# Layout of a DRAM scratch tensor in a CIN tower: one 8 KB row per partition for the loads, eight 512-byte rows per partition for the stores

## The reference

```python
e = stack([tbl_f[ids[:, f]] for f in range(64)], axis=1)        # 512 x 64 x 16
x = e; outs = []
for W, b in ((W0, b0), (W1, b1), (W2, b2)):
    z = einsum('bhd,bfd->bhfd', x, e).reshape(B, h * f, d)
    x = einsum('oc,bcd->bod', W, z) + b[None, :, None]
    outs.append(x.sum(axis=2))
h = concatenate(outs + [dense_ctx], axis=1)
y = relu(relu(h @ W_top1 + b_top1) @ W_top2 + b_top2) @ W_top3
```

## Time and profile before

| | |
|---|---|
| median of 3 runs | 1180.73 us (1180.33 to 1181.44) |
| the profiled execution's own time | 1183.49 us |
| its span in the trace | 1181.5 us |
| busy share PE / DVE / POOL / ACT | 95% / 84% / 77% / 58% |
| mean granted clock of TensorE | 0.994 |
| transfers: packets, bytes | 103836, 142.87 MB |

### The profile page before, as it was taken

One profiled execution on the slowest core, in us unless ns is written; L12 is line 12 of the kernel. 1 busy time (PEld: TensorE's weight loads), 2 busy tenths in 40 slices (PEclk: granted clock), 3 DMA queues, 4 the chain that ended last, 5 costly groups with the idle time before them and its releaser, 6 DMA issues.

```text
span 1181.5 us, 13928 instructions
## 1 busy us (share of the span) xinstructions
PE 1117.9 (95%) x4276; PEld 745.3 (63%) x4276; DVE 997.4 (84%) x652; ACT 681.9 (58%) x695; POOL 905.2 (77%) x403
## 2 busy tenths in 40 slices
PE   0499999999999999999999999999999999999998
PEld 0256666666666666676666666666666666667685
DVE  4589899989998989899899989898998999896542
ACT  5256465665656656656656566566566665654533
POOL 6459998889988888888899888888898996575000
PEclk9999999999999999999999999999999999999999
DMA  6542424234252524252342525241523425242991
GB/s 240 170 130 65 113 74 150 65 120 121 77 155 74 157 74 140 68 152 66 109 131 71 160 74 157 74 140 64 146 76 104 136 69 160 73 152 94 294 297 46
DMA packets 103836, 142.87 MB, mean 121 GB/s; under 512 B 11745, under 2 KB 55009, under 8 KB 103042
## 3 DMA queue, kind: packets, MB, share of 16 engines
q1 hardware_dynamic: 95618, 140.42, 39.3%
q0 software_dynamic: 8192, 2.11, 2.2%
HBM read 114.96 MB, written 27.53 MB: 121 GB/s over the span
## 4 chain that ended last, share of the span: by engine, by line
PE 83%; POOL 4%; issue 3%; DMA 3%; SPq 2%; ACT 2%; DVE 1%; ACTq 0%
PE acc L1085 50%; PE acc L1079 26%; POOL z_lo L580 3%; PE turn_gram_ps L1153 3%; DMA z_float<-gram_scratch 2%; PE acc L1108 1%; POOL emb L571 1%; ACT x L878 1%; DMA z<-gram_scratch 1%; PE z_ps L1214 1%; PE turn_gram_ps L1140 1%; DMA land<-x_scratch 1%; ACT z_hi L1046 0%; DVE z_lo L816 0%; SPq L512 0%
## 5 line engine op out<-in xcount | busy, mean ns | idle before, releaser
L580 POOL TENSOR_TENSOR z_lo<-z,z_hi 128x2048 fp32r<-128x2048 f32 x143 | 659.5, 4613 | 116.8 <-ACT z_hi L849 110.3
L1085 PE MATMUL acc<-z_hi,w_hi 128*128 128x512 f32 x896 | 379.0, 423 | 6.8 <-DVE z_lo L659 4.2
L1079 PE MATMUL acc<-z_float,w_sb 128*128 128x512 f32 x768 | 349.1, 601 | 8.2 <-ACT x L878 7.6
L1085 PE MATMUL acc<-z_hi,w_lo 128*128 128x512 f32 x896 | 354.6, 396 | 0.0
L1085 PE MATMUL acc<-z_lo,w_hi 128*128 128x512 f32 x896 | 354.3, 395 | 0.0
L849 ACT ACTIVATE z_hi<-z 128x2048 fp32r<-128x2048 f32 x144 | 275.1, 1910 | 53.6 <-DVE z L647 53.6
L571 POOL DMA_INDIRECT emb<-in_tables,rows_chunk x256 | 245.4, 959 | 63.3 <-issue 51.8
L1079 PEld LDWEIGHTS acc<-z_float,w_sb 128*128 128x128 f32 x768 | 144.4, 191 | 174.6 <-issue 166.4
L858 ACT ACTIVATE z_hi<-z_ps 128x1024 fp32r<-128x1024 f32 x160 | 164.9, 1031 | 135.9 <-PE acc L1085 108.9
L659 DVE TENSOR_TENSOR z_lo<-z_ps,z_hi 128x1024 fp32r<-128x1024 f32 x160 | 194.9, 1218 | 45.3 <-ACT z_hi L858 45.3
L647 DVE TENSOR_TENSOR z<-operand_even,x_shift 128x2048 f32<-128x2048 f32 x80 | 183.0, 2287 | 37.3 <-PE acc L1085 16.6
(11 more groups left out here) (112 smaller groups left out, 640.7 us busy)
## 6 DMA issues: line engine op xcount, KB each, us to landing
land<-x_scratch SPq DMA_DIRECT2D x128, 256.0 KB
land<-x_scratch SPq DMA_DIRECT2D x128, 128.0 KB
x_shift<-x_scratch SPq DMA_DIRECT2D x16, 1024.0 KB, 5.8
gram_scratch<-gram SPq DMA_DIRECT2D x32, 512.0 KB
x_shift<-x_scratch SPq DMA_DIRECT2D x16, 768.0 KB
z_float<-gram_scratch SPq DMA_DIRECT2D x7, 1024.0 KB, 10.8
x_scratch<-emb SPq DMA_DIRECT2D x32, 192.0 KB
x_shift<-gram_scratch SPq DMA_DIRECT2D x6, 1024.0 KB, 9.2
```

The source lines that it names most:

```text
L580: pool.tensor_tensor(z_lo[:, slot], z[:, slot], z_hi[:, slot].bitcast(F32), ALU.subtract).then_inc(subtracted, 1)
L1079: mm = pe.matmul(acc[:, :], weights[:, tile0 + q, :], z_float[:, g.float_slot(pos), q, :], start=start and q == 0, stop=stop and q == QUAD ...
L1085: mm = pe.matmul(acc[:, :], w[:, tile, :], zz[:, slot, q, :], start=False, stop=stop and n == 2)
```

## The change

The scratch tensor in DRAM gets another order of dimensions. Before, each partition (channel h) had for each of the 32 chunk halves all 64 fields. After, each partition has for each of the 8 blocks of fields all 32 chunk halves. Both tensors have the same size, and the step from one partition to the next is the same, 128 KiB. The store of a half has the same bytes from the same buffer, but its 4096 bytes per partition now go to 8 places in DRAM, 16 KiB apart. The load of a block has the same bytes to the same buffer, but its 8192 bytes per partition now come from one place rather than from 16 places 4 KiB apart. Nothing else changes: order, waits, semaphores, buffers and arithmetic stay.

```diff
-    gram_scratch = nc.dram_tensor("gram_scratch", (HID, 2 * CHUNKS, FIELDS, HALF_B), F32, kind="Internal").ap()
+    gram_scratch = nc.dram_tensor("gram_scratch", (HID, HALF_BLOCKS, 2 * CHUNKS, F_BLOCK * HALF_B), F32, kind="Internal").ap()
@@ store_gram
-                offset, = at(c.count(2 * FIELDS * HALF_B, half * FIELDS * HALF_B))
+                offset, = at(c.count(2 * F_BLOCK * HALF_B, half * F_BLOCK * HALF_B))
                 wait_all((gram_staged, c.count(BLOCKS, 2 * half + 2)))
                 sp.dma_start(bass.AP(gram_scratch.tensor, offset,
-                                     [[2 * CHUNKS * FIELDS * HALF_B, HID], [1, FIELDS * HALF_B]]),
-                             gram[:, :, :].rearrange("p f b -> p (f b)")).then_inc(gram_stored, 16)
+                                     [[2 * CHUNKS * FIELDS * HALF_B, HID], [2 * CHUNKS * F_BLOCK * HALF_B, HALF_BLOCKS],
+                                      [1, F_BLOCK * HALF_B]]),
+                             gram[:, :, :].rearrange("p (k f) b -> p k (f b)", f=F_BLOCK)).then_inc(gram_stored, 16)
@@ load_gram
-                sp.dma_start(gram_buffers[k % GRAM_BUFFERS].rearrange("p c f b -> p c (f b)"), bass.AP(
-                    gram_scratch.tensor, (half * CHUNKS * FIELDS + fb * F_BLOCK) * HALF_B,
-                    [[2 * CHUNKS * FIELDS * HALF_B, HID], [FIELDS * HALF_B, CHUNKS], [1, F_BLOCK * HALF_B]],
+                sp.dma_start(gram_buffers[k % GRAM_BUFFERS].rearrange("p c f b -> p (c f b)"), bass.AP(
+                    gram_scratch.tensor, (fb * 2 + half) * CHUNKS * F_BLOCK * HALF_B,
+                    [[2 * CHUNKS * FIELDS * HALF_B, HID], [1, CHUNKS * F_BLOCK * HALF_B]],
                 )).then_inc(gram_loaded[k % GRAM_BUFFERS], 16)
```

## The result

The changed kernel takes 1173.72 us (median of 4 runs, 1172.88 to 1173.98) against 1181.09 us of the kernel before in the same session (1180.33 to 1181.76): a ratio of 0.9936, 95% interval 0.9923 to 0.9948. The profiled execution took 1172.88 us, with a span of 1170.9 us. The lines of the new kernel have moved by one behind the store: L1225 is what L1224 was, L1047 what L1046 was, L513 what L512 was.

What follows compares the result with a forecast made beforehand. PE bounds the rounds, the saturated load queue the last layer. Faster loads give 5.3 us less 0.1 for handovers, stores nothing: 1180.73 less 5.2 gives 1175.5 us (profiled 1183.49 to 1178.3), range 1174.3 to 1179.5.

Steps and rivals of the forecast that it cites:

- What bounds the last layer, and what comes next: Last layer: the saturated DMA queue bounds it at 290 GB/s; with faster loads PE sets the end, at 1160.9 us.
- The load at 2.5 us: Last layer's 16 scratch loads: each takes 2.5 us in 8192-byte rows, against 3.62 us at 290 GB/s.
- together 45.5 us: PE's work in the last layer from the first split block: 12 split blocks of 3.20 us plus two plain, 7.1 us.
- 5.3 us, is all that faster loads can give: Last layer: PE's 50.8 us less 45.5 us of its own work, the upper limit of the gain.
- about 0.9 us of slow clock: Last layer: part of the 5.3 us, beside 4.4 us of gaps; PE's clock was 0.62 between 1136 and 1140.
- The stores: 32 gram stores, rounds and last layer: 1.8 to 2.5 us each, +0.4 to +1.1, bound +2.1; nothing on the total.
- Are the loads early enough: Last layer's reloads: at 5.5 us from issue to landing, blocks 13 to 15 are ready before PE wants them.
- rival B: Last layer: reloads take 10.6 us to land, blocks 13 and 14 come late; 1177 to 1178.4 us; 12%.
- Rival A: Last layer: loads get no faster, the queue stays the bound; 1180.7 to 1184 us, middle 1181.7; 12%.
- Rival C: Rounds: slower stores before the x1 store reach PE, about 1 us in each of 14 rounds; +9, 1190 us; 7%.
- my reading of its cover: Rounds: 2.7 us spare at ACT's copy of the first shift load, so stores up to 4.1 us cost nothing.
- The range: Whole kernel: 1174.3 to 1179.5 us, about 8 in 10; the forecast's own range 1174.5 to 1176.8, at most 5.3 gained.

Runs made afterwards that it cites:

- e3: Against the kernel before: only the load changed, one 8 KB row per partition, store as before; ratio 0.9936, last layer 64.11 us.
- e5: Against the kernel before: 512-byte rows kept, but 13 of 16 loads bring only half their bytes; 1175.26 against 1183.15 us, ratio 0.9936.
- e9: Against the changed kernel: stores in 4096 rows of 128 bytes, loads still 8 KB rows; ratio to the kernel before 0.9969, last layer 67.18 us.
- e1: The kernel before run once more without edit; ratio 0.9999, last layer 72.30 us.
- e4: Against the kernel before: new store in 1024 rows of 512 bytes, loads in 512-byte rows from other places; ratio 1.0018, last layer 73.68 us.
- e6: Against the kernel before: store as before, loads in 8 rows of 1 KB per partition; ratio 0.9931, last layer 65.28 us.
- e10: Against the changed kernel: stores in 8192 rows of 64 bytes, loads still 8 KB rows; ratio to the kernel before 1.0055, last layer 78.20 us.
- e2: The changed kernel run once more without edit; 1173.24 against 1181.62 us, ratio 0.9934, last layer 65.78 us.

## Why the prediction was right or wrong

**What bounds the last layer, and what comes next: right.** The queue was the bound, and PE took its place. e3 and e5 show both, one by longer rows for the same bytes, one by half as many rows and bytes.

**The load at 2.5 us: right** (2.49).

**The step that failed: "together 45.5 us", PE's own work from the first split product on.** It was mis-sized. The same stretch, from the start of the first split product (1112.92) to the end of the last (1155.59), measures 42.7 us in the changed kernel, and 42.1 of it lie behind the end of L1241. So "5.3 us, is all that faster loads can give" was too little: it is 50.8 - 42.7 = 8.1. I took 3.20 us per split block from the last block of the trace before, which PE had begun after a wait. A wait costs more than the idle time that the records show. The kernel before, at the first wait:

```profile
1121.41 0.29 PE L1224 MATMUL z_ps<-z_lo,w_hi 128*128 128x256 f32 x1
1121.53 0.28 PE L1224 MATMUL z_ps<-z_hi,w_lo 128*128 128x256 f32 x1
1122.20 0.39 PE L1224 MATMUL z_ps<-z_hi,w_hi 128*128 128x256 f32 x1 [0.39 <-DVE z_lo L816]
1122.43 0.28 PE L1224 MATMUL z_ps<-z_lo,w_hi 128*128 128x256 f32 x1
1122.55 0.29 PE L1224 MATMUL z_ps<-z_hi,w_lo 128*128 128x256 f32 x1
```

In a run of products each lasts 0.28 us by the records but they start 0.12 apart, so they overlap. The last one before a wait has nothing to overlap with (0.16 us), and the first after it lasts 0.39 and has the next 0.23 behind it rather than 0.12 (0.11 us). One restart costs 0.27 us by these rows, and 3.19 - 2.93 = 0.26 by the blocks of e9. Twelve blocks make 3.1 us and the plain pair 0.2 (6.91 for 7.12), less 0.5 because the first product (1115.39 in the earlier trace rows) overlapped the end of L1240: 2.8 of the 2.9 us that were missing.

**A second term was too small: "about 0.9 us of slow clock".** It was what the sum left over. The trace before shows it directly. From 1135.64 on the products start 0.21 us apart:

```profile
1135.27 0.29 PE L1224 MATMUL z_ps<-z_lo,w_hi 128*128 128x256 f32 x1
1135.39 0.29 PE L1224 MATMUL z_ps<-z_hi,w_lo 128*128 128x256 f32 x1
...
1136.07 0.42 PE L1224 MATMUL z_ps<-z_hi,w_hi 128*128 128x256 f32 x1
1136.28 0.41 PE L1224 MATMUL z_ps<-z_lo,w_hi 128*128 128x256 f32 x1
```

There are 14 such steps up to 1138.63, 1.3 us more than at 0.12, and the plain pair behind them is 0.2 longer from start to start than in the changed kernel: 1.5 us. Of the 8.1 us, 4.4 are then waits, 8 x 0.26 = 2.1 restarts and 1.5 slow clock. The second trace of the kernel before (e1) has the fall at the same place (0.65 between 1134 and 1138). The same count fits e4, whose windows after the first split product show a clock of 1.00: 6.8 + 11 x 0.26 = 9.7 us over the floor, measured 9.6. No run took the slow clock away alone, and a gap does not bring it by itself: e4's longest gap there was 2.4 us, e9's 2.1, and the clock stayed at 1.00.

**The stores: right in size, but not all of their delay was counted.** I took +0.4 to +1.1 us. Between 200 and 1000 us the shortest time of a store from issue to landing is 2.7 us in e3 and 3.6 in the changed kernel, and SP's wait for the x1 store, which runs behind one, grew by 0.6. But SP also takes longer to issue (0.64 us for the store rather than 0.37, 1.40 for the two x1 stores rather than 0.91), so that the shift loads of the round shown start 1.5 us later. That was hidden too. In the last layer they are hidden beside fast loads (e3 against the changed kernel), and cost 1.4 in all beside loads in 512-byte rows (e4).

**Are the loads early enough: right in the outcome, wrong in a time.** I used 5.5 us from issue to landing; in the changed kernel L513 has

```profile
DMA to landing us min/median/max: 4.8/8.2/11.7
```

so the median lies midway between my 5.5 and rival B's 10.6. B did not come about: block 13's load is issued at 1134.56, into an almost empty queue (share 0.43 between 1133 and 1137), those of 14 and 15 follow at 1138.0 and 1138.4, and ACT waited for PE, not for them. (The queue had less time to spare than the fifth that I took: 2.49 us per load against PE's 2.93, 15%.)

**Rival A fell** with e3 and e6. With it falls, for this kernel, the Trainium skill's figure (DMA: Bandwidth & Descriptors, Specifications) of 512 bytes as enough for line rate: the loads moved 290 GB/s in rows of 512 bytes, 348 in 1 KB, 390 in 2 KB and 422 to 426 in 8 KB. The Trainium skill (the same page, Why small descriptors are slow) counts a fixed cost of some 3 cycles per packet beside one cycle for each 32 bytes. An estimate from these figures for 512 bytes is 3 of 19; the runs show a fixed 9.6 of 28.3 ns.

**Rival C fell, and my reading of its cover with it.** I read 2.7 us from one pair of instructions. In e10 the shift loads are issued 4.9 us later than before and ACT waits for them 41 times, but the rounds lose 1.4 us in all, and none behind the fourth; the lead that DVE and PE have takes up the rest. The place where slow stores do count is the last layer, at its beginning, where store, copy and store follow each other (e9, e10).

**The range** failed at its lower end because it was built on the same 5.3 us as an upper limit for the gain. (That limit and the 0.5 us for the runs' spread give 1174.9, not the 1174.5 that stands there; the true limit of 8.1 gives 1172.1.)

## What to carry to other kernels

Read an engine's own floor from a run of its instructions without gaps, not from one group that follows a wait: the cost of a gap is its idle time and a restart (here 0.26 us), and where gaps go, both go. A strided DRAM load costs by its rows as well as by its bytes; price it from two row lengths in the traces, and compare the result with what the consumer needs, for beyond that (here 2.93 us per MB) longer rows bring nothing. Moving short rows from a load that somebody waits for to a store that nobody waits for paid here; what cover the store has is seen by making it slower, better than by reading the slack of one instruction.

## What the hardware showed that I had not expected

A row of a DRAM load costs a fixed time beside its bytes: 28.3, 47.0 and 84 ns per row and engine for 512, 1024 and 2048 bytes, and 311 ns (2.49 us over 8 rows) for 8192, close to 9.6 ns plus 0.0365 ns per byte in all four. Stores of gram cost the 14 rounds nothing down to rows of 128 bytes, and 1.4 us in all at 64. And the granted clock of TensorE fell to 0.50 for a window in which PE's records show no idle time (e2), which cost 1.7 us; why it fell stays open.
